# GpSimd instead of SyncE issues the row and result transfers of the experts, with longer rings for rows and weights

## The chip, the cores and the metric

The kernel runs on one core of a Trainium2 chip. The metric is the device time of one execution in microseconds (us). Three runs of the kernel before gave 1716.96 us as the median (1716.13 to 1722.56). The profile is of one more execution, of 1711.19 us, whose traced span is 1709.2 us.

## The reference, cut to what matters

Four layers follow each other on x of shape (4, 512, 128), each adding an attention and a feed-forward part of the normalized x. The last two feed-forward parts are mixtures of experts: a shared expert for all 2048 tokens, and the best 4 of 32 (layer 2) or 2 of 16 (layer 3) routed ones for each token.

```
# layer 2: E = 32 experts of width 96, best 4
act = silu(x @ w_gate[e]) * (x @ w_up[e]);  eo = act @ w_down[e]
routed = sum over the token's 4 experts of combine[t, e] * eo[t, e]
# layer 3: E = 16 experts of width 256, best 2, with biases
h = silu(x @ W1[e] + b1[e]) * (x @ W11[e] + b11[e]);  y += (h @ W2[e] + b2[e]) * gates[t, e]
```

## The kernel before, in words

Each engine has its own program, written out by hand; they meet only through semaphores (`wait_ge`). In layers 2 and 3 all engines walk the same list of steps: `both` counts n, the step of attention, and four quarters i of each; a "slot" below is one such quarter (4n + i). In a slot TensorE makes one 128x512 score tile whose row maximum VectorE takes (L1486), one more whose exponential ScalarE takes (L1927), and part of the product with V. Layer 3's attention starts 64 steps behind that of layer 2. Beside these, `plan` places the expert work in slots, and each engine runs its share of a slot's tasks in the plan's order, so an engine that waits for one task holds up all that stands behind it in its own program.

The expert work goes like this. After routing, GpSimd scatters the normalized tokens by indirect DMA into a DRAM list `xd`, sorted by expert in tiles of 128 rows (L2143; 64 transfers in layer 2, 32 in layer 3). Layer 2 has 96 such tiles, two to an item, layer 3 has 48, one to an item; so each layer has 48 routed items, behind the items of the shared expert. For each routed item:

- "rows": SyncE loads two tiles of `xd` into a buffer of the ring `XG` of 4 pairs (L2377), once the tile that stood there has been transposed (`XTURN`, L2376). The first four pairs are loaded by GpSimd in `first_rows` (L2151), right after the scatter.
- "turned": TensorE transposes the rows (L942), ScalarE copies them out (L1912).
- "hidden": TensorE multiplies with the expert's gate and up weights, which stand in the ring `WR` of 6 items (layer 2) or 5 items (layer 3), numbers held in `ahead` (L371). Then ScalarE and VectorE gate the result (L1906, L1452, L1454).
- "down": TensorE multiplies with the down weights; then SyncE loads the weights of the item `ahead` further on (`item_weights`, L2331; it waits for `DOWN` of this item, reads the expert's number from SBUF, and issues one transfer per tile). ScalarE copies the result to `YOs` (L1918), and SyncE, having waited for that copy (`YO_A`, L2384), writes it to the DRAM list `yd` (L2385).

When all results have landed, GpSimd gathers them back by indirect DMA (L2134) and VectorE adds them to X (L1473).

SyncE's program also holds the loads of the attention: six transfers of `stack` for every four steps (L2260, L2262), and the writes of `split_out` (L2243, L2246), three times a layer for the batches 1 to 3. GpSimd's program also has the scatter, the four operations of `part_of` per batch (L2089 to L2097), and the gathers.

## Time and profile before

| | |
|---|---|
| median of three runs | 1716.96 us (1716.13 to 1722.56) |
| profiled execution | 1711.19 us, span 1709.2 us |
| TensorE matmul busy | 1268.7 us (74%) |
| VectorE busy | 1246.9 us (73%) |
| ScalarE busy | 921.7 us (54%) |
| GpSimd busy | 307.0 us (18%) |

The span falls in stretches with different limits, so the shares over the whole say little about one of them. The routed items of layer 2 run from 918 to about 1090 us, those of layer 3 from 1415 to about 1612 us. SyncE has no busy time in the page; its queue of issued transfers is read from the timeline of engine SP. The chain of work that ended last gives at each step what released it; "DMA RA<-xd" there is a transfer from its issue to its landing.

### The profile page before, as it was taken

The numbers are of one execution on the slowest core, as the hardware profiler recorded it, in microseconds if no ns is written. First come the engines' busy times: TensorE is split into PE (matmuls) and PEld (weight loads), VectorE is DVE, ScalarE is ACT, GpSimd is POOL, SyncE is SP. The second block draws the span as 40 slices with busy tenths as digits, with TensorE's granted clock in tenths as the row PEclk, the third lists the DMA queues.
The fourth block names the chain that finished last, engine by engine and source line by source line (L and its number), as shares of the span: only waits on it lengthen the run. The fifth ranks groups of instructions, "written<-read, shape, count | busy, mean of one in ns | idle before, by whom it ended". The sixth has DMA issues, their size and how long they took to land.

```text
span 1709.2 us, 24192 instructions
## 1 busy us (share of the span) xinstructions
PE 1268.7 (74%) x7198; PEld 678.4 (40%) x7198; DVE 1246.9 (73%) x4139; ACT 921.7 (54%) x2172; POOL 307.0 (18%) x418
## 2 busy tenths in 40 slices
PE   6988979887432334256788999877899879987976
PEld 2444545444211112131145656422565435665522
DVE  5997979988789999868565666667677755544563
ACT  2898988886354444412344556544444445544545
POOL 0111102002000000004654001166110250100051
PEclk6999999899755555556889999988998989998989
DMA  3010101100392000012313666523110234545420
GB/s 114 24 70 6 51 24 32 49 1 1 111 329 81 6 6 11 2 46 86 121 53 100 182 179 180 157 75 64 46 31 27 80 68 140 149 101 159 117 67 23
DMA packets 171850, 135.40 MB, mean 79 GB/s; under 512 B 75218, under 2 KB 149271, under 8 KB 171667
## 3 DMA queue, kind: packets, MB, share of 16 engines
q1 hardware_dynamic: 163561, 119.83, 24.1%
q0 software_dynamic: 6528, 13.64, 2.9%
q8 instruction: 58, 0.95, 0.2%
q14 instruction: 71, 0.58, 0.1%
q10 hardware_dynamic: 1632, 0.39, 0.1%
HBM read 95.96 MB, written 47.27 MB: 84 GB/s over the span
## 4 chain that ended last, share of the span: by engine, by line
PE 41%; DVE 36%; issue 8%; ACT 6%; DMA 4%; SPq 2%; another core or an unknown queue 2%; POOL 1%; DVEq 0%; ACTq 0%
PE PS L575 36%; DVE nmx L1486 6%; DVE RA L1731 6%; DVE RA L1735 4%; PE PS L571 4%; DVE RA L1289 4%; DVE RA L1292 3%; DMA RA<-xd 2%; DMA RA<-wd 1%; DVE RB L1289 1%; ACT RA L1877 1%; PE PS L942 1%; DVE RB L1292 1%; DMA RA<-scr 1%
## 5 line engine op out<-in xcount | busy, mean ns | idle before, releaser
L575 PE MATMUL PS<-RA 125*128 125x512 bf16 (+6 forms) x2368 | 552.2, 347 | 105.2 <-DVE nmx L1486 63.0
L1486 DVE TENSOR_REDUCE nmx<-PS 128x1 f32<-128x512 f32 x512 | 346.4, 684 | 260.7 <-PE PS L575 224.4
L1927 ACT ACTIVATE RA<-PS 128x512 f32<-128x512 f32 x512 | 295.5, 599 | 251.5 <-PE PS L575 200.7
L575 PEld LDWEIGHTS PS<-RA 125*128 125x128 bf16 (+4 forms) x2368 | 230.0, 132 | 372.8 <-DVE nmx L1486 144.3
L575 PE MATMUL PS<-RA,Vs 128*32 128x512 f32 x1240 | 201.6, 646 | 0.7 <-ACT RA L1927 0.7
L2053 ACT ACTIVATE RA<-RA 128x8 f32<-128x8 f32 x511 | 107.5, 210 | 142.5 <-DVE RA L1731 142.3
L571 PE MATMUL PS<-ident,RB 128*128 128x128 f32 (+2 forms) x331 | 61.3, 329 | 157.6 <-DVE RB L1664 141.4
L2134 POOL DMA_INDIRECT RA<-yd,RA x96 | 94.8, 987 | 274.6 <-DMA yd<-RB 217.9
L1289 DVE TENSOR_SCALAR RA<-PS 128x1024 f32<-128x1024 f32 x96 | 116.9, 1218 | 21.9 <-PE PS L575 20.9
L1877 ACT ACTIVATE RA<-RA,nm 128x512 f32<-128x512 f32 x192 | 128.8, 725 | 1.1 <-POOL nm L2208 0.9
L1292 DVE CUSTOM_DVE_ANT_0 RA<-RA,RB 128x512 f32<-128x512 f32 x192 | 125.1, 688 | 3.3
L571 PE MATMUL PS<-ident,RA 128*128 128x128 f32 x768 | 107.8, 285 | 26.3 <-ACT RA L1883 17.5
L571 PEld LDWEIGHTS PS<-ident,RB 128*128 128x128 f32 (+2 forms) x331 | 43.8, 164 | 192.2 <-DVE RB L1664 113.1
L1906 ACT ACTIVATE RA<-PS 128x256 f32<-128x256 f32 (+1 forms) x144 | 55.1, 382 | 112.6 <-PE PS L575 107.0
L2143 POOL DMA_INDIRECT xd<-XN,RA x96 | 93.4, 973 | 123.5 <-DVE sd L1416 52.7
L571 PEld LDWEIGHTS PS<-ident,RA 128*128 128x128 f32 x768 | 89.1, 144 | 61.0 <-ACT RA L1883 28.6
L2089 POOL CAST parts<-QK 128x1024 bf16<-128x1024 f32 x6 | 6.2, 1037 | 549.8 <-DVE ms L1245 549.8
L1731 DVE TENSOR_TENSOR_SCAN RA<-RA 128x16 f32<-128x16 f32 x512 | 95.5, 187 | 7.0 <-ACT RA L2053 1.6
L1735 DVE COPY RA<-RA 128x4 f32<-128x4 f32 x512 | 86.3, 169 | 15.1 <-DVE RA L1731 0.4
L575 PE MATMUL PS<-RB 128*128 128x352 f32 (+2 forms) x88 | 60.2, 842 | 36.7 <-ACT RB L2027 23.3
L575 PE MATMUL PS<-RB,RA 128*96 128x128 f32 (+1 forms) x576 | 83.0, 281 | 2.8 <-DVE RA L1454 2.8
L2208 POOL TENSOR_SCALAR nm<-mx 128x2 f32<-128x2 f32 x128 | 27.3, 214 | 319.7 <-DVE mx L1292 269.7
(308 smaller groups left out, 1923.8 us busy)
## 6 DMA issues: line engine op xcount, KB each, us to landing
RA<-scr SPq DMA_DIRECT2D x288, 96.0 KB
RA<-wd SPq DMA_DIRECT2D x48, 384.0 KB
RA<-wd SPq DMA_DIRECT2D x96, 160.0 KB
xd<-Otok SPq DMA_DIRECT2D x36, 256.0 KB, 3.3
RA<-xd SPq DMA_DIRECT2D x64, 128.0 KB, 3.2
scr<-parts SPq DMA_DIRECT2D x48, 128.0 KB
yd<-RB SPq DMA_DIRECT2D x48, 128.0 KB, 2.7
wd<-in_L_ffn_W SPq DMA_DIRECT2D x2, 2048.0 KB, 14.9
```

The costliest lines, as they stand in the source:

```text
L571: ins = e.transpose(bank[bk][0:s.shape[-1], j * 128:j * 128 + s.shape[0]], s, ident[0:s.shape[0], 0:s.shape[0]])
L575: return e.matmul(o, l, r, start=first, stop=last)
L1289: e.tensor_scalar(Y[n % 4][:, 2 * u:2 * u + 2, :], PS[:, 2 * u:2 * u + 2, :], C0, -C0, ALU.min, ALU.max).then_inc(*CLIP.up("clip", n, u))
L1292: ins = e.tensor_tensor_reduce(out=Y[n % 4][:, qt, :], in0=Y[n % 4][:, qt, :], in1=Dk[:, qt, :], scale=1.0, scalar=NEG, op0=ALU.mult, op1= ...
L1486: e.tensor_reduce(nmx[:, (g + lx) % 3, c:c + 1], bank[(6, 0)[i % 2]], AX.X, ALU.max, negate=True).then_inc(*ROWMAX.up(layer, n, i))
L1731: e.tensor_tensor_scan(sc, RA[:, 16 * t:16 * t + 16], RA[:, 8192 + 16 * t:8192 + 16 * t + 16], 0.0, ALU.mult, ALU.subtract).then_inc(*SCAN ...
L1735: e.tensor_copy(D1[:, t + 1, :, 0], sc.rearrange("p (b e) -> p b e", e=4)[:, :, 2]).then_inc(*CARRY.up(t))
L1877: e.activation(Y[m % 4][:, qt, :], Y[m % 4][:, qt, :], ACT.Exp, bias=nm[:, m % 4, qt:qt + 1]).then_inc(*EXP.up(0, m, qt))
L1927: e.activation(chunk(layer, k, i), bank[(1, 5)[i % 2]], ACT.Exp).then_inc(*EXP.up(layer, k, i))
L2053: e.activation(D1[:, t + 1, :, 1:3], sv[:, :, 3:4].broadcast_to([128, 4, 2]), ACT.Tanh).then_inc(*TANH.up(t + 1))
L2134: e.indirect_dma_start(XG[:, i % 6 // 2, i % 2, :], None, yd[lx], bass.IndirectOffsetOnAxis(ap=IDX[:, n, j:j + 1], axis=0)).then_inc(*GATH ...
L2143: e.indirect_dma_start(xd[lx], bass.IndirectOffsetOnAxis(ap=IDX[:, n, j:j + 1], axis=0), XN[:, n, :], None).then_inc(*SCAT.up(lx, "all"))
```

## The change

GpSimd's `expert_step` takes over the tasks "rows" and the storing half of "down" from SyncE's, with the same waits and the same slots; SyncE keeps the weights. The ring of row pairs grows from 4 to 6 and is filled by six transfers in `first_rows`; the plan asks for rows later in number (the pair 6 ahead of the one freed) in the same slots. The ring of weights grows to 11 items in layer 2 and 9 in layer 3; the added buffers lie in `RB`, and `weights` fills the longer rings at the start of each layer, one task a slot in layer 2 and two in layer 3. The computation is the same.

```diff
-    topk, ntiles, nexps, ffs, groups, ahead = (4, 2), (NT2, NT3), (32, 16), (96, 256), (2, 1), (6, 5)
+    topk, ntiles, nexps, ffs, groups, ahead = (4, 2), (NT2, NT3), (32, 16), (96, 256), (2, 1), (11, 9)
@@ the plan of the expert steps
-            r = G * (i - nsh + 6)
-            fetch = [("rows", r)] if i >= first and end > nsh and r >= 8 and r % 2 == 0 and r < ntiles[lx] else []
+            r = G * (i - nsh) + 12 + 4 * (G - 1)
+            fetch = [("rows", r)] if i >= first and end > nsh and r >= 12 and r % 2 == 0 and r < ntiles[lx] else []
@@ pool_program
         def expert_step(lx, task):
+            if name == "rows":
+                r = task[1]
+                u = r // 2 % 6
+                pool.wait_ge(SCAT, lx, "all")
+                pool.wait_ge(XTURN, lx, nsh + (r - 11) // G)
+                e.dma_start(XG[:, u, :, :], xd[lx][128 * r:128 * r + 256, :].rearrange("(t p) d -> p t d", p=128)).then_inc(*XGIN[u].up(lx, r // 2))
+            elif name == "down" and task[1] >= nsh:
+                i = task[1]
+                r = G * (i - nsh)
+                pool.wait_ge(YO_A, lx, i)
+                e.dma_start(yd[lx][128 * r:128 * r + 128 * G, :].rearrange("(t p) d -> p t d", p=128),
+                            YOs[lx][:, i % 6, :].rearrange("p (t d) -> p t d", d=128)).then_inc(*YOUT[i % 6].up(lx, i))
...
@@ first_rows
-            for u in range(4):
+            for u in range(6):
@@ sp_program
         def expert_step(lx, task):
-            if name == "rows":
...
-            elif name == "down" and task[1] >= nsh:
+            if name == "down" and task[1] >= nsh:
                 i = task[1]
-                r = G * (i - nsh)
                 if i + ahead[lx] < items[lx]:
                     item_weights(lx, i + ahead[lx])
-                sp.wait_ge(YO_A, lx, i)
-                e.dma_start(yd[lx]...
```

## Rows read from the trace of the kernel before

**Rows 1.** Stretches: us, busy PE PEld DVE ACT POOL, clock, DMA share, GB/s

```profile
915.00:1112.00 197.00, 177.37 (x1186) 109.77 (x1186) 118.86 (x282) 111.39 (x265) 16.95 (x17) 0.99 0.60 170
1410.00:1625.00 215.00, 190.64 (x1352) 126.08 (x1351) 115.33 (x267) 106.55 (x272) 9.27 (x8) 0.97 0.48 132
```

**Rows 2.** TensorE's waits, 915 to 1112: waited for, total us, times, longest

```profile
PE PS L942 <- DMA RA<-xd: 7.7, 4, 4.9
```

**Rows 3.** TensorE's waits, 1410 to 1625

```profile
PE PS L575 <- DMA RA<-wd: 7.0, 6, 2.1
PE PS L942 <- DMA RA<-xd: 5.0, 3, 3.9
PE PS L942 <- DVE Otok L1216: 4.3, 4, 1.4
```

**Rows 4.** TensorE's wait for the first rows, 1410 to 1420

```profile
PE PS L942 <- DMA RA<-xd: 0.6, 1, 0.6
```

**Rows 5.** SyncE's queue about 1030: start us, us, line, operation, count

```profile
1025.32 1.19 SPq L2331 DMA_DIRECT2D RA<-wd  x2
1026.57 0.42 SPq L2385 DMA_DIRECT2D yd<-RB  x1
1027.05 0.79 SPq L2260 DMA_DIRECT2D RA<-scr  x1
...
1031.53 0.44 SPq L2377 DMA_DIRECT2D RA<-xd  x1
```

**Rows 6.** The chain that ended last: start us, us, what

```profile
1031.53 7.74 DMA RA<-xd
...
1559.59 8.70 DMA RA<-wd
```

**Rows 7.** TensorE's timeline about 1560, with idle time before and releaser

```profile
1555.06 1.29 PE L575 MATMUL PS<-RA 128*128 128x128 f32 x8 [1.50 <-DMA RA<-wd]
...
1560.71 1.44 PE L575 MATMUL PS<-RA 128*128 128x128 f32 x12
...
1567.51 0.45 PE L942 MATMUL PS<-ident,RA 128*128 128x128 f32 x1 [3.94 <-DMA RA<-xd]
1568.42 2.79 PE L575 MATMUL PS<-RA 128*128 128x128 f32 x12 [0.47 <-DMA RA<-wd]
```

**Rows 8.** Busy time and clock in three stretches of 5 us (columns of rows 1)

```profile
1555.00:1560.00 5.00, 4.94 (x28) 3.18 (x28) 0.94 (x2) 1.77 (x4) 0.00 (x0) 0.66 0.42 137
1565.00:1570.00 5.00, 2.02 (x8) 1.66 (x9) 0.24 (x1) 0.27 (x1) 0.00 (x0) 0.61 0.84 258
1570.00:1575.00 5.00, 5.00 (x28) 3.02 (x28) 1.76 (x4) 2.05 (x5) 0.00 (x0) 0.71 0.30 69
```

**Rows 9.** TensorE's transposes of layer 2's, then layer 3's items: min/median/max ns, first and last

```profile
L942 PE MATMUL PS<-ident,RA x96: 270/273/445, 918.1 to 1087.1; 128*128 128x128 f32 x96
L942 PE MATMUL PS<-ident,RA x48: 272/274/447, 1415.3 to 1610.8; 128*128 128x128 f32 x48
```

**Rows 10.** GpSimd's own transfers, by line: min/median/max ns

```profile
L2151 POOL DMA_DIRECT2D RA<-xd x8: 727/756/807, 915.5 to 1412.9; - x8
...
DMA to landing us min/median/max: 2.5/3.6/6.2
```

**Rows 11.** GpSimd's timeline about 1024: start us, us, operation, idle before

```profile
1024.37 1.03 POOL L2089 CAST parts<-QK 128x1024 bf16<-128x1024 f32 x1 [105.88 <-DVE ms L1245]
...
1028.79 2.13 POOL L2097 TENSOR_TENSOR parts<-QK,parts 128x1024 bf16<-128x1024 f32 x1
```

**Rows 12.** SyncE's queue, at the start of both layers' weights

```profile
833.13 4.89 SPq L2331 DMA_DIRECT2D RA<-wd  x6
844.96 0.76 SPq L2260 DMA_DIRECT2D RA<-scr  x1
...
1356.42 3.78 SPq L2331 DMA_DIRECT2D RA<-wd  x5
```

**Rows 13.** The chain that ended last, between 849 and 860

```profile
849.96 3.35 another core or an unknown queue
854.71 4.33 another core or an unknown queue
```

More of the change, by code:

```diff
@@ L202, in build @@
     SG = RA[:, 8416:8432]
-    XG = RA[:, 8448:9472].rearrange("p (u t k) -> p u t k", u=4, t=2)
-    HB = RA[:, 9728:10240].rearrange("p (u k) -> p u k", u=2)
-    XGTs = (RB[:, 11008:11520].rearrange("p (u k) -> p u k", u=2), RA[:, 9472:9728].rearrange("p (u k) -> p u k", u=2))
-    WR = (RA[:, 18432:22272].rearrange("p (u g k) -> p u g k", u=6, g=2), RA[:, 18432:22272].rearrange("p (u g k) -> p u g k", u=5, g=1))
+    XG = RA[:, 8448:9984].rearrange("p (u t k) -> p u t k", u=6, t=2)
+    HB = RA[:, 10240:10752].rearrange("p (u k) -> p u k", u=2)
+    XGTs = (RB[:, 11008:11520].rearrange("p (u k) -> p u k", u=2), RA[:, 9984:10240].rearrange("p (u k) -> p u k", u=2))
+    WR = ([x[:, i:i + 640].rearrange("p (g k) -> p g k", g=2) for x, a, n in ((RA, 18432, 6), (RB, 6944, 5)) for i in range(a, a + 640 * n, 640)],
+          [x[:, i:i + 768].rearrange("p (g k) -> p g k", g=1) for x, a, n in ((RA, 18432, 5), (RB, 9216, 4)) for i in range(a, a + 768 * n, 768)])
     YOs = (RB[:, 0:1536].rearrange("p (u k) -> p u k", u=6), RB[:, 5504:6272].rearrange("p (u k) -> p u k", u=6))
@@ L246, in build @@
     W2S, W3S, TABLE = loads("w2s"), loads("w3s"), loads("table")
-    WIN = [loads(f"win{i}") for i in range(6)]
+    WIN = [loads(f"win{i}") for i in range(11)]
     B3, SEL, B2IN, B2UP, B2DN, B3UP, B3DN = (loads(n) for n in ("b3", "sel", "b2in", "b2up", "b2dn", "b3up", "b3dn"))
@@ L252, in build @@
     SCAT = loads("scatter")
-    XGIN = [loads(f"xg{i}") for i in range(4)]
-    XGFIRST = [loads(f"xgfirst{i}") for i in range(4)]
+    XGIN = [loads(f"xg{i}") for i in range(6)]
+    XGFIRST = [loads(f"xgfirst{i}") for i in range(6)]
     YOUT = [loads(f"yout{i}") for i in range(6)]
@@ L911, in expert_step @@
                 else:
-                    w = WR[lx][:, (i - nsh) % ahead[lx], :, :]
+                    w = WR[lx][(i - nsh) % ahead[lx]]
                     pe.wait_ge(WIN[(i - nsh) % ahead[lx]], lx, i)
@@ L937, in expert_step @@
                     r = G * (i - nsh) + g
-                    if r < 8:
+                    if r < 12:
                         pe.wait_ge(XGFIRST[r // 2], lx)
                     else:
-                        pe.wait_ge(XGIN[r // 2 % 4], lx, r // 2)
-                    ins = e.transpose(bank[2][:, 128 * g:128 * g + 128], XG[:, r // 2 % 4, r % 2, :], ident[:, :])
+                        pe.wait_ge(XGIN[r // 2 % 6], lx, r // 2)
+                    ins = e.transpose(bank[2][:, 128 * g:128 * g + 128], XG[:, r // 2 % 6, r % 2, :], ident[:, :])
                 ins.then_inc(*XTURN.up(lx, i))
@@ L961, in expert_step @@
                         lhs = HB[0:m, i % 2, 128 * (nc_ * g + c):128 * (nc_ * g + c) + 128]
-                        w = shared[lx][i][3][c] if i < nsh else WR[lx][0:m, (i - nsh) % ahead[lx], g, 2 * f + 128 * c:2 * f + 128 * c + 128]
+                        w = shared[lx][i][3][c] if i < nsh else WR[lx][(i - nsh) % ahead[lx]][0:m, g, 2 * f + 128 * c:2 * f + 128 * c + 128]
                         ins = mm(o, lhs, w, c == 0 and lx == 0, c == nc_ - 1)
@@ L2121, in expert_step @@
             name, k = task[0], topk[lx]
-            if name == "gather":
+            nsh, G = len(shared[lx]), groups[lx]
+            if name == "rows":
[4 more added lines that the diff above has]
+                e.dma_start(XG[:, u, :, :], xd[lx][128 * r:128 * r + 256, :].rearrange("(t p) d -> p t d", p=128)).then_inc(*XGIN[u].up(lx, r // 2))
+                XGIN[u].mark(lx, "all")
+            elif name == "down" and task[1] >= nsh:
[4 more added lines that the diff above has]
+                            YOs[lx][:, i % 6, :].rearrange("p (t d) -> p t d", d=128)).then_inc(*YOUT[i % 6].up(lx, i))
+                YOUT[i % 6].mark(lx, "all")
+            elif name == "gather":
                 i = task[1]
@@ L2149, in first_rows @@
                 pool.wait_ge(XW, "routed", 0, 16 * topk[0] - 1)
-            for u in range(4):
+            for u in range(6):
                 e.dma_start(XG[:, u, :, :], xd[lx][256 * u:256 * u + 256, :].rearrange("(t p) d -> p t d", p=128)).then_inc(*XGFIRST[u].up(lx))
@@ L2370, in expert_step @@
             name = task[0]
[L2371 to L2379 removed]
+            nsh = len(shared[lx])
+            if name == "down" and task[1] >= nsh:
                 i = task[1]
[L2381 removed]
                 if i + ahead[lx] < items[lx]:
                     item_weights(lx, i + ahead[lx])
[L2384 to L2387 removed]
         xin = T["L0_attn_x"].rearrange("b s d -> (b s) d").rearrange("(n p) d -> p n d", p=128)
```

12 lines of the change are left out of this document (1 added, 11 removed).

## The prediction

> **What bounds the kernel now.** I read first the busy time by stretch [rows 1]. The two stretches in which the routed items run, 915 to 1112 and 1410 to 1625 us, have TensorE busy 177.4 of 197 and 190.6 of 215 us, at a granted clock of 0.99 and 0.97, while VectorE and ScalarE are busy 50 to 60% of either and GpSimd 17 and 9 us in all. So TensorE sets the pace there, and what can be won without less matmul work is its idle time: 19.6 and 24.4 us. These stretches hold all that the change moves, apart from the first loads.
>
> Next I read what TensorE waited for in them [rows 2, 3]. The reader is to see two kinds of rows. Waits for a transfer: 7.7 us for rows (RA<-xd) in layer 2; 7.0 us for weights (RA<-wd) and 5.0 us for rows in layer 3. And waits for other engines, such as 4.3 us for Otok in layer 3 which the change doesn't touch. Not all row waits are SyncE's: the longest of layer 2, 4.9 us, is the one for the first rows (GpSimd's first row load starts at 915.5, the first transpose at 918.1) [rows 2, 9, 10], and 0.6 us in layer 3 is the same [rows 4]. Both come out of the scatter and `first_rows`, which are GpSimd's already.
>
> Why are SyncE's transfers late? Its queue about 1030 us shows it [rows 5]. One item costs it 0.44 us for rows, 1.19 us for two weight transfers and 0.42 us for the result, and then the six loads of `stack` follow in its program, from 1027.05 to 1031.53, 4.48 us in which nothing of the experts is issued. The row load at 1031.53 stands right behind. The chain of work has this very transfer on it for 7.74 us, and one of weights in layer 3 for 8.70 us [rows 6]: it lands slowly since stack loads of the same queue are ahead of it, and SyncE comes back to the items late. The ring of 4 pairs and the ring of 5 weights are too short for such a delay and landing together.
>
> **The change part by part.**
>
> 1. Row loads leave SyncE's queue and are asked for 6 pairs ahead. An item of layer 2 takes (1087.1 - 918.1)/47 = 3.60 us, one of layer 3 (1610.8 - 1415.3)/47 = 4.16 us [rows 9]. Six pairs are about 21 us of lead in layer 2, where one pair is one item; in layer 3, where a pair serves two items, the load is asked for ten items before its use, about 41 us. The longest landing of GpSimd's own eight row loads is 6.2 us [rows 10]. That covers it several times. Gone: in layer 2, 7.7 - 4.9 = 2.8 us; in layer 3, 5.0 - 0.6 = 4.4 us.
>
> 2. Weights stay with SyncE, 11 and 9 items ahead, which is 39 and 37 us of lead against a burst of about 4.5 us plus a landing of 8.7 [rows 5, 6]. The writes of `split_out` hold SyncE too, in groups of at most six transfers, which would have to take 20 us each time to use up that lead. Gone: 7.0 us in layer 3 [rows 3]; in layer 2 no weight wait stands among TensorE's waits.
>
> 3. The clock. Within 1553 to 1568 us TensorE waited for a weight and for a row, and right behind it the granted clock is 0.66, 0.61 and 0.71, a mixture of the full 2.4 GHz and of 1.2 GHz [rows 8]. Twelve matmuls that take 1.44 us before the stall take 2.79 us behind it [rows 7]. The work that a full clock would have saved is busy time by what is missing: 4.94 x 0.34 + 2.02 x 0.39 + 5.00 x 0.29 = 1.7 + 0.8 + 1.5 = 3.9 us. The fall followed these waits, so it goes with them.
>
> 4. GpSimd's new work: 60 row loads, 96 results and 4 more first rows, 160 instructions at 0.756 us [rows 10] and a gap of about 0.3, some 170 us, in stretches where it is busy 17 and 9 us [rows 1]. In layer 2 one item costs it 2 x 1.06 = 2.1 of 3.60 us. Cover holds unless an issue takes more than 1.5 us. The page of rows has no case above 0.807 us for this kind.
>
> 5. The waits that GpSimd now has. `XTURN` and `YO_A` tie it to the slots; behind them stand its own next tasks: `part_of` for batch 3. Before, these four ran in one go as soon as VectorE's maximum was there, from 1024.37 to 1030.9 [rows 11]; now they stand in four slots four apart, 12 slots, some 27 us, from first to last. The write that needs them comes three slots behind the last, and behind a stack burst of 4.5 us. I cost this at nothing; if the cover fails, it is one SyncE wait of about 3 us that no weight with 39 us of lead feels. Who waits for GpSimd's results is ScalarE's copy six items later (21 us) and the first gather. Cost 0, from 0 to 3 us.
>
> 6. The longer first fill: five more items in layer 2 and four in layer 3. At 4.89/3 = 1.63 us an item SyncE is busy until 833.13 + 8 x 1.63 = 846.2 where its next stack load stood at 844.96; in layer 3, 9 x 3.78/5 = 6.8 us from 1356.42, so until 1363.2 [rows 12]. The load delayed by 1.2 us is wanted some 16 slots later. But two pauses of 3.35 and 4.33 us stand on the chain there with an unknown releaser [rows 13]; the first comes right behind the burst of six stack loads that begins at 844.96. 1.6 MB more about 840 us might bring one more or lengthen one, or shift them off. Bounds -4 to +8 us, value taken 0, since the second comes with no burst right before it.
>
> The sum: 2.8 + 4.4 + 7.0 + 3.9 = 18.1 us off. Since TensorE is the bound before and behind each stall, I let nothing be taken back by the next wait; that is the optimistic end, and half is the other (9 us). The profiled execution would go from 1711.19 to 1693.1 us (span 1709.2 to 1691.1). It lies 5.8 us below the median of the three runs, so on the median: 1716.96 - 18.1 = 1698.9, rounded to 1699.
>
> A page speaks against the change. GpSimd's row loads were issued in 0.727 to 0.807 us each while VectorE ran its reductions from PSUM [rows 10]. The Trainium skill, page "SBUF — State Buffer", section "SBUF: two separate sides", says that a transfer issued by GpSimd has its descriptors written by GpSimd's cores, which are shut out while VectorE runs an SBUF-to-SBUF operation in its fast mode on two ports; its advice is to issue from SyncE or ScalarE. By that rule alone the change would be a loss. The operations that VectorE runs in these stretches read PSUM or are tiny, and the trace's eight loads and their spread of 80 ns show nothing of such a lock.
>
> **The rivals.**
>
> A. Others take back the stall (chance 0.20). While TensorE waited for a row, Otok and the gates were finishing too; 4.3 us of Otok waits remain in layer 3 [rows 3], and they may grow when TensorE arrives earlier. For it: each slot has a round trip to VectorE. Against it: VectorE is idle for 40% of both stretches. Half the gain stays: 1717 - 9 = 1708, just at the edge of what counts as no change.
>
> B. The first fill brings pauses (0.13). Two more pauses of the kind in rows 13 cost 2 x 4.3 = 8.6 us, four cost 17 (one for each burst of the two fills, and one behind each): 1708 to 1716.
>
> C. GpSimd becomes the bound (0.07), the slower side. Place: the 48 items of layer 2. Price: if one issue costs as much as GpSimd's longest operation in the row, 2.13 us [rows 11], with the gap 2.43, an item costs it 4.86 against 3.60 us: 48 x 1.26 = 60 us, less the 21.6 us that six buffers absorb, 38 us. Layer 3 has one and a half issues an item, 3.65 below 4.16, and keeps its gain of 15. Time: 1716.96 + 38 - 15 = 1740. It decides from 1.5 us an issue. The lock of the page above would act here. Against it: rows 10.
>
> D. The change doesn't do what it says would need that the waits come from full transfer engines and not from the queue; the DMA share is 0.60 and 0.48 [rows 1], so over some 37 us of lead it can't last. I put it into A.
>
> **How the numbers follow.** Forecast (0.60): all four terms, 1699, its own range 1694 to 1706. A 0.20 at 1708, B 0.13 at 1708 to 1716, C 0.07 at 1740. The range takes A and B whole and a few us of spread of the median (its three runs span 6.4 us), and leaves out C: 1690 to 1718. A measurement of this kernel can tell about 0.5%, 8.6 us. Faster by more: the forecast and part of A and B, 0.66. Within: the rest of A and B, 0.25. Slower: C and a rest, 0.09.
>
> **What would show it.** In the profile after: TensorE's waits for RA<-wd gone in the second stretch, those for RA<-xd left with the first rows alone (about 5 and 0.6 us); no clock below 0.9 about 1550 to 1575; GpSimd busy 50 to 70 us more in each of the two stretches, with row loads of 0.75 us; SyncE waiting for DOWN in front of most weights. The stretch of layer 2 shorter by 3 us, that of layer 3 by 15. The prediction is wrong if issues take over 1.5 us, if Otok waits grow by the same sum, or if the stretch from 820 to 870 us gets longer.

## The result, and the profile after

The changed kernel takes 1698.28 us as the median of six runs (1695.56 to 1703.93); six runs of the kernel before, taken beside them and before them, have 1716.55 us (1711.11 to 1722.56). The ratio is estimated from all these runs at 0.9889, with an interval of 0.9868 to 0.9911 (the quotient of the two medians alone is 0.9894): faster by 18.3 us. The forecast was 1699 us. One run of the kernel before, in the third series below, took 2111.86 us in a slow state, and the ratios leave it out.

| | before | after |
|---|---|---|
| median of six runs | 1716.55 us | 1698.28 us |
| profiled execution, its span | 1711.19, 1709.2 us | 1701.65, 1699.9 us |
| TensorE matmul busy | 1268.7 us | 1257.0 us |
| VectorE, ScalarE busy | 1246.9, 921.7 us | 1249.4, 921.7 us |
| GpSimd busy | 307.0 us | 413.1 us |
| layer 2's items, first to last transpose | 169.0 us | 169.9 us |
| layer 3's items, first to last transpose | 195.5 us | 179.0 us |

The two profiled executions differ by 9.5 us only, half of what the medians do: that of before lay 5.4 us below its median, that of after 3.4 us above. So the sum of the prediction must be read against the stretches, not against the two spans. Lines of the kernel after stand one or 16 lower than before: L942 is now L943, SyncE's weight loads L2347, GpSimd's row loads L2129 and results L2135, and the first rows L2167.

TensorE's waits of the kernel after, in the same two windows as [rows 2, 3], 915 to 1112 and 1410 to 1625 us (waited for, total us, times, longest):

```profile
PE PS L943 <- DMA RA<-xd: 5.2, 1, 5.2
PE PS L943 <- DVE Otok L1217: 4.3, 3, 2.2
...
PE PS L943 <- DVE Otok L1217: 4.8, 4, 1.4
PE PS L576 <- DVE nmx L1487: 4.2, 2, 3.9
...
PE PS L576 <- DMA RA<-mT: 0.4, 1, 0.4
```

In layer 2 one wait for rows is left, the one for the first rows. In layer 3 no wait for rows or weights stands in the answer; the only transfer waited for is one of mT, 0.4 us. The wait of 3.9 us for nmx (a row maximum) isn't at the items: it ends at 1413.5, ahead of the first transpose of layer 3. The transposes themselves (duration ns min/median/max, first and last start), to be laid beside [rows 9]:

```profile
L943 PE MATMUL PS<-ident,RA x96: 270/273/449, 921.4 to 1091.3; 128*128 128x128 f32 x96
...
L943 PE MATMUL PS<-ident,RA x48: 272/274/477, 1423.4 to 1602.4; 128*128 128x128 f32 x48
```

An item of layer 3 takes 179.0/47 = 3.81 us where it took 4.16; one of layer 2 takes 169.9/47 = 3.61, as before. Busy time and clock of the kernel after in the stretches of [rows 1] and in four of 5 us (columns: PE, PEld, DVE, ACT, POOL busy, clock, DMA share, GB/s):

```profile
915.00:1112.00 197.00, 177.94 (x1157) 111.06 (x1175) 116.06 (x274) 108.71 (x259) 84.69 (x109) 0.97 0.51 154
1410.00:1625.00 215.00, 195.61 (x1382) 127.66 (x1409) 124.43 (x289) 113.89 (x287) 58.69 (x86) 0.98 0.46 131
...
1555.00:1560.00 5.00, 4.95 (x38) 3.21 (x38) 3.87 (x8) 3.23 (x9) 1.80 (x3) 1.00 0.58 119
...
1565.00:1570.00 5.00, 5.00 (x41) 3.56 (x42) 3.19 (x7) 3.04 (x9) 1.08 (x2) 1.00 0.80 223
1570.00:1575.00 5.00, 4.30 (x38) 3.49 (x41) 2.88 (x10) 2.29 (x9) 0.54 (x1) 1.00 1.02 299
```

TensorE stays at the full 2.4 GHz where the kernel before had 0.66, 0.61 and 0.71 [rows 8]. GpSimd's busy time in the two stretches went from 17 and 9 us to 85 and 59. Its transfers, of the kernel after (duration of one on GpSimd's queue, ns min/median/max, then the landings of the rows and of the results):

```profile
L2129 POOL DMA_DIRECT2D RA<-xd x60: 712/720/750, 922.9 to 1562.8; - x60
...
DMA to landing us min/median/max: 2.5/3.6/6.5
...
L2135 POOL DMA_DIRECT2D yd<-RB x96: 538/650/731, 934.4 to 1611.9; - x96
...
DMA to landing us min/median/max: 1.8/3.4/6.6
```

A row load takes 0.720 us of GpSimd where the prediction, from eight of them, took 0.756, and the spread over 60 is 38 ns. The Trainium skill, page "DMA: Bandwidth & Descriptors", section "Anatomy of one DMA — SWDGE (gpsimd) path", gives a fit for a transfer issued by GpSimd of 2.0 us and the bytes at 436 GB/s; 128 KB would be 2.3 us by it, an estimate. The trace has 2.5 us for the fastest of these 60, 3.6 in the median and 6.5 for the slowest: here the fit lies just under the fastest, and a lead has to be sized by the slowest.

### The profile page after: what moved, and what is told of

It reads as the page before. It is cut to its first block, busy times and chain, and to the rows that moved or that the text cites. A ratio compares the mean times of both kernels' runs of the same rounds, so it can differ in the third digit from the quotient of the medians.

```text
span 1699.9 us, 24108 instructions
## 1 busy us (share of the span) xinstructions
PE 1257.0 (74%) x7112; PEld 673.3 (40%) x7198; DVE 1249.4 (74%) x4139; ACT 921.7 (54%) x2172; POOL 413.1 (24%) x578
## 4 chain that ended last, share of the span: by engine, by line
PE 43%; DVE 37%; issue 7%; ACT 6%; another core or an unknown queue 3%; DMA 2%; POOL 1%; SPq 1%; ACTq 0%; DVEq 0%
PE PS L576 38%; DVE nmx L1487 6%; DVE RA L1732 6%; DVE RA L1736 4%; PE PS L572 4%; DVE RA L1290 4%; DVE RA L1293 3%; DVE RB L1290 1%; PE PS L943 1%; DVE RB L1293 1%; ACT RA L1878 1%; DVE Otok L1217 1%; ACT RA L1928 1%; DVE RA L1455 1%
## 5 line engine op out<-in xcount | busy, mean ns | idle before, releaser
L576 PE MATMUL PS<-RA 128*128 128x512 bf16 (+6 forms) x1963 | 505.7, 354 | 104.6 <-DVE nmx L1487 69.1
L576 PEld LDWEIGHTS PS<-RA 128*128 128x128 bf16 (+4 forms) x2048 | 193.9, 122 | 367.2 <-DVE nmx L1487 148.5
L576 PE MATMUL PS<-RA,Vs 128*32 128x512 f32 x1240 | 205.2, 657 | 3.5 <-ACT RA L1928 1.0
L572 PE MATMUL PS<-ident,RA 128*128 128x128 f32 x768 | 107.1, 284 | 26.5 <-ACT RA L1884 17.7
L2135 POOL DMA_DIRECT2D yd<-RB x96 | 61.1, 637 | 202.3 <-ACT RB L1919 199.1
L576 PE MATMUL PS<-RB 128*96 128x128 f32 (+3 forms) x248 | 83.1, 484 | 34.5 <-ACT RB L2028 21.1
```

Of the source, the lines that this page charges most:

```text
L572: ins = e.transpose(bank[bk][0:s.shape[-1], j * 128:j * 128 + s.shape[0]], s, ident[0:s.shape[0], 0:s.shape[0]])
L576: return e.matmul(o, l, r, start=first, stop=last)
```

## The experiments

The question that the result leaves is which half of the change does it. Theory 1 (that of the prediction): a transfer comes late because it stands in SyncE's queue behind others, and what removes the wait is lead, so the rings decide and the issuer matters little. Theory 2: the issuer decides, since GpSimd has a queue with nothing else in it. The kernels ran in three series. The kernel before had medians of 1670.72 us in the first (26 runs), 1718.99 in the second (20) and 1670.01 in the third (11), so only ratios within a series are compared; what differs between the series is told at the end. As above, a ratio is an estimate from all runs of both kernels, and need not be the quotient of the two medians.

| kernel | issuer of rows, results | rings: pairs, weights, results | us | ratio, interval |
|---|---|---|---|---|
| series 1: after_again | GpSimd | 6, 11/9, 6 | 1651.61 | 0.9890 (0.9862 to 0.9919) |
| rings_alone | SyncE | 6, 11/9, 6 | 1658.73 | 0.9920 (0.9891 to 0.9948) |
| issuer_alone | GpSimd | 4, 6/5, 6 | 1664.67 | 0.9963 (0.9940 to 0.9987) |
| weights_ring_alone | SyncE | 4, 11/9, 6 | 1666.71 | 0.9988 (0.9962 to 1.0015) |
| series 2: before_again | SyncE | 4, 6/5, 6 | 1716.54 | 0.9992 (0.9973 to 1.0011) |
| rings_results | SyncE | 6, 11/9, 6/10 | 1692.01 | 0.9849 (0.9822 to 0.9876) |
| later_rows | GpSimd | 6, 11/9, 6 | 1706.15 | 0.9927 (0.9901 to 0.9953) |
| filler3 | GpSimd, with more work | 6, 11/9, 6 | 1735.36 | 1.0087 (1.0056 to 1.0118) |
| series 3: after_third | GpSimd | 6, 11/9, 6 | 1650.19 | 0.9897 (0.9873 to 0.9920) |
| rings_results_again | SyncE | 6, 11/9, 6/10 | 1647.17 | 0.9875 (0.9841 to 0.9909) |
| gpsimd_results_ring | GpSimd | 6, 11/9, 6/10 | 1652.21 | 0.9905 (0.9884 to 0.9927) |
| gpsimd_results_only | SyncE rows, GpSimd results | 6, 11/9, 6 | 1650.10 | 0.9878 (0.9850 to 0.9906) |

What these kernels spend where, from the first and last starts of three lines in each profile. The first column of times is from VectorE's first row maximum of layer 2's attention to the first transpose of layer 2's rows; then layer 2's items, first to last transpose; then the stretch between, from there to the first transpose of layer 3's rows; then layer 3's items; last, from the last transpose of layer 3 to the end of the span:

```
                       to layer 2's items   items 2   between   items 3   behind
before                       161.9           169.0     328.2     195.5     98.4
after                        167.7           169.9     332.1     179.0     97.5
after_again                  147.7           170.1     309.4     180.4     86.6
rings_alone                  146.8           172.8     307.5     187.1     87.8
issuer_alone                 146.9           170.6     302.9     193.9     87.4
weights_ring_alone           145.8           171.3     311.4     193.5     86.0
before_again                 161.1           172.5     325.0     196.9     99.4
rings_results                160.6           170.1     325.5     179.2     98.8
later_rows                   169.2           169.0     334.4     181.8     96.7
filler3                      165.2           195.7     343.1     178.5     96.0
after_third                  146.5           170.1     304.6     179.7     87.4
rings_results_again          148.7           170.3     301.1     180.1     87.3
gpsimd_results_ring          148.8           170.5     308.0     180.0     87.5
gpsimd_results_only          147.0           169.9     311.7     179.9     88.0
```

### after_again: the change once more, beside its halves

No edit: the kernel after.

> The changed kernel once more, for a second profile. Its first profile is only 9.3 us shorter than that of the kernel before, the medians differ by 18.3 us. In it the items of layer 3 gave 16.5 us, but the stretch from the first score tile of layer 2 to its first routed transpose took 167.7 instead of 161.9 us, and the items of layer 2 took 169.9 instead of 169.0 us. Theory 1 (the loss in the first stretch is the price of the longer first fill of weights): 166 to 169 us again, with pauses of an unknown releaser of together about 15 us between 820 and 870. Theory 2 (such pauses fall differently in every execution, and the profiles were a long and a short one): the stretch lies anywhere from 160 to 168 us. The ratio to the kernel before is 0.989 in both.

Measured 1651.61 us, 0.9890: the ratio is that of the first measurement, though all kernels are some 46 us shorter here. The stretch to layer 2's items took 147.7 us, which neither theory had: there are no pauses in this profile, as the last section tells. The items of layer 3 take 180.4 us. This is the yardstick of the series.

### rings_alone: the longer rings, SyncE still issues everything

```diff
 pool_program, expert_step
-            if name == "rows":
...
 sp_program, expert_step
+            if name == "rows":
+                sp.wait_ge(XTURN, lx, nsh + (r - 11) // G)
+                e.dma_start(XG[:, u, :, :], xd[lx]...
+            elif name == "down" and task[1] >= nsh:
+                sp.wait_ge(YO_A, lx, i)
+                e.dma_start(yd[lx]...
```

> The longer rings (6 pairs, 11 and 9 weights) with SyncE as the issuer of rows and results, as before. Theory 1 (the stall is SyncE's burst plus a slow landing against too little lead; lead cures it by itself): TensorE's waits for weights 0 and for rows only the first ones (about 5 us and 0.6 us), items of layer 3 in 179 to 182 us, ratio 0.989 to 0.991. Theory 2 (what matters is that SyncE's queue is too full, so that it falls behind for good): row waits of over 2 us stay in layer 2, layer 3's items above 186 us, ratio 0.994 or more.

Measured 1658.73 us, 0.9920: most of the gain, but the items of layer 3 take 187.1 us and not 180.4. Theory 1 is right about the waits for rows and weights and wrong about the items, for which theory 2 has the right number (above 186 us) and not the reason. TensorE's waits in layer 3, 1372 to 1570 us, have no wait for weights, and for rows only the first; a new one stands beside it. The rows below are, in turn, TensorE's waits, ScalarE's wait about 1525 to 1550, two copies of ScalarE, two stores of SyncE, and TensorE's timeline behind:

```profile
PE PS L943 <- DMA RA<-xd: 4.1, 1, 4.1
PE PS L576 <- ACT RB L1919: 4.1, 1, 4.1
...
ACT RB L1919 <- DMA yd<-RB: 6.4, 2, 5.7
...
1513.35 0.27 ACT L1919 COPY RB<-PS 128x128 f32<-128x128 f32 x1 [0.17 <-PE PS L576]
...
1539.38 0.27 ACT L1919 COPY RB<-PS 128x128 f32<-128x128 f32 x1 [5.74 <-DMA yd<-RB]
...
1517.82 3.19 SPq L2248 DMA_DIRECT2D scr<-parts  x2
...
1532.16 0.41 SPq L2387 DMA_DIRECT2D yd<-RB  x1
...
1539.70 2.82 PE L576 MATMUL PS<-RA 128*128 128x128 f32 x12 [4.08 <-ACT RB L1919]
```

The copy at 1513.35 is the 31st of layer 3, and the store at 1532.16 is the 31st of SyncE: a result was finished at 1513.62 and stood for 18.5 us before SyncE came to it, behind the writes of `split_out`, the six stack loads and the tasks that these had put off. The 37th copy needs that place, since the ring has 6. It comes at 1539.38, 7.2 us behind the issue. So a third ring became the shortest. The twelve matmuls behind this wait take 2.82 us, as in the stall of the kernel before [rows 7].

Layer 2's items take 2.7 us more here than in after_again, with the same waits of TensorE but for the first rows (4.9 and 5.3 us). There the granted clock differs: what it lacks costs 7.6 us here and 4.5 in after_again, by the working of "3, the clock" below.

### issuer_alone: GpSimd issues, the rings as before

```diff
-    ... groups, ahead = ..., (2, 1), (11, 9)
+    ... groups, ahead = ..., (2, 1), (6, 5)
-            for u in range(6):
+            for u in range(4):
 (and % 4 for % 6 where the pairs are counted)
```

> GpSimd issues rows and results, the rings stay 4 pairs, 6 and 5 items. Theory 1 (lead): the waits for rows go, since the load is no longer behind the stack burst and lands in at most 6.2 us against 14 us of lead; the waits for weights in layer 3 stay in part, 2 to 5 us of 7.0, since SyncE's bursts still stand before them; items of layer 3 in 183 to 189 us, ratio 0.992 to 0.995. Theory 2 (the queue): both kinds of waits go, 179 to 182 us, ratio 0.989.

Measured 1664.67 us, 0.9963. TensorE's waits in layer 3, 1372 to 1570 us, and the longest of them:

```profile
PE PS L576 <- DMA RA<-wd: 8.0, 4, 5.6
PE PS L943 <- DMA RA<-xd: 4.4, 1, 4.4
...
1530.08 2.79 PE L576 MATMUL PS<-RA 128*128 128x128 f32 x12 [5.61 <-DMA RA<-wd]
```

With rows and results gone from its queue SyncE is still late with the weights: 8.0 us of waits against 7.0 before [rows 3]. All row waits but the first are gone. A shorter queue alone doesn't do what lead does. Theory 1 had the kinds of waits right and was too hopeful in all its numbers (2 to 5 us of weight waits, 183 to 189 us of items, 0.992 to 0.995, where 8.0, 193.9 and 0.9963 were measured).

### weights_ring_alone: only the ring of weights is longer

```diff
 against the kernel before:
-    ... groups, ahead = ..., (2, 1), (6, 5)
+    ... groups, ahead = ..., (2, 1), (11, 9)
```

> Only the rings of weights are longer (11 and 9 items); 4 pairs of rows, SyncE issues all. Theory 1 (lead): waits for weights 0, waits for rows stay at 2.8 us in layer 2 and 4.4 us in layer 3 beside the first ones; items of layer 3 in 186 to 190 us, ratio 0.993 to 0.996. Theory 2 (the rows were late because of the weights' own waits in the queue): row waits go as well, ratio 0.989 to 0.991.

Measured 1666.71 us, 0.9988: no gain that can be told. The same view, same window:

```profile
PE PS L943 <- DMA RA<-xd: 17.7, 5, 6.7
```

The waits for weights are gone, and the waits for rows behind the first have grown from 4.4 us (5.0 less 0.6, [rows 3, 4]) to 11.0 (17.7 less the 6.7 of the first rows). Weights and rows together were 7.0 + 4.4 = 11.4 us in the kernel before, so nearly nothing is gone. The delay in SyncE's queue is one; whichever ring is the shortest shows it. That is a new wait in the place of the one removed, and neither theory had it (theory 1: 4.4 us of row waits, 186 to 190 us of items, 0.993 to 0.996, where 193.5 us and 0.9988 were measured). It is why half a change was worth next to nothing: GpSimd as issuer alone is worth 0.4%, the weights' ring alone 0.1%, both rings alone 0.8%, everything 1.1%. The ring of pairs alone wasn't run. Nor was the plan alone: in layer 3 the kernel before asks for a row load four items before its use (`G * (i - nsh + 6)`), where the changed one asks ten before, and its four pairs were free two items earlier than it asked. So some 8 us of the new lead of the rows there could have been had without a longer ring; what they are worth isn't known.

### before_again: the kernel before, profiled in the second series

No edit. It gives series 2 a profile of the kernel before.

> The kernel before once more, for a profile from the same chip as its variants. Theory 1 (the pauses of unknown releaser belong to the chip and not to the change): they are there or missing in this profile as in the others of its chip, and the stretches outside the routed items agree with the changed kernel's within 2 us each; the items of layer 3 take 193 to 197 us with 10 to 14 us of waits for transfers besides the first rows. Theory 2 (the change's longer first fill or GpSimd's transfers cause or lengthen them): the stretch up to layer 2's first transpose is 3 us or more shorter here than in the changed kernel. Ratio 1.000.

Measured 1716.54 us, 0.9992. Its items take 172.5 us in layer 2, where the first profile of the same kernel has 169.0. So the same kernel differs by 3.5 us in this stretch from one execution to the next, more than the 2.8 us that step 1 forecast for it. Layer 3's 196.9 us are within theory 1's 193 to 197, and the stretch to layer 2's items, 161.1 us, is within a microsecond of the first profile of this kernel. It is 6.6 us shorter than in the kernel after, and that is the sign of theory 2. rings_results below, with the long fill and 160.6 us, clears the fill of it; the rest of the question is for the last section.

### rings_results: SyncE issues everything, and the ring of results is longer too

```diff
 against rings_alone:
-    YOs = (..., RB[:, 5504:6272].rearrange("p (u k) -> p u k", u=6))
+    YOs = (..., RB[:, 5504:6784].rearrange("p (u k) -> p u k", u=10))
+    yring = (6, 10)
-                if i - nsh >= 6:
-                    act.wait_ge(YOUT[i % 6], lx, i - 6)
+                k = yring[lx]
+                if i - nsh >= k:
+                    act.wait_ge(YOUT[i % k], lx, i - k)
```

> SyncE issues everything, as before, with the longer rings of rows and weights, and layer 3's ring of results is lengthened from 6 to 10 as well. In the profile of the long rings without it, the one wait left was ScalarE's for a result's landing (5.7 us, passed on to TensorE as 4.1 us). Theory 1 (each stall is the shortest lead among the three rings, whoever issues): that wait goes, layer 3's items take 179 to 183 us instead of 187, ratio 0.988 to 0.991, so that GpSimd as the issuer is not needed. Theory 2 (GpSimd as the issuer has a worth of its own): another wait takes its place, 185 to 188 us, ratio 0.991 to 0.994.

Measured 1692.01 us, 0.9849. Its layer 3 items take 179.2 us, as in the kernel after, with GpSimd doing nothing for them. The rows are TensorE's wait for transfers in layer 2 (916.5 to 1090 us) and the first two rows of its waits about layer 3's items (1400 to 1590 us). The 5.0 us of "issue" lie ahead of the first transpose, which starts at 1412.1; among the items one transfer is still waited for, a weight, for 0.2 us:

```profile
PE PS L944 <- DMA RA<-xd: 5.0, 1, 5.0
...
PE PS L577 <- issue: 5.0, 2, 4.3
PE PS L944 <- DVE Otok L1218: 3.4, 3, 1.4
```

The comparison with before_again is the cleanest of all, since both are of one series and their other stretches agree within 1.1 us: items of layer 2 shorter by 2.4 us, of layer 3 by 17.7, the spans by 21.1 (1711.2 to 1690.1). Theory 1 stands: once all three rings have lead, the issuer isn't needed. The ratio is better than its range (0.988 to 0.991).

### later_rows: the change, with the first rows wanted three slots later

```diff
+            if not lx and i == nsh - 2:
+                steps += [[] for _ in range(4)]
-    last = spread(2, expert_steps(0, 0), 68, 1.15)
+    last = spread(2, expert_steps(0, 0), 68, 1.2)
-    last = spread(3, expert_steps(1, 1), READY3[3] + 71 - 4 * LEAD, 1.05)
+    last = spread(3, expert_steps(1, 1), READY3[3] + 74 - 4 * LEAD, 1.05)
```

> The changed kernel with the first routed transposes three slots later in both layers (four empty steps and a rate of 1.2 instead of 1.15 in layer 2, a start of 74 instead of 71 in layer 3), because the first rows are what is left of TensorE's waits for transfers: 5.3 and 6.2 us. Theory 1 (TensorE has attention work to do in those three slots): both waits fall under 1.5 us, ratio 0.982 to 0.986 to the kernel before, that is 5 to 10 us better than the change. Theory 2 (the slots behind are as full and only the wait moves): the waits are gone but the stretches give it back, ratio 0.988 to 0.990.

This goes for the 5.2 us that are left. Measured 1706.15 us, 0.9927: no gain beside the change, if anything a loss, and outside the ranges of both theories. In layer 2, 920 to 1095 us, TensorE waited

```profile
PE PS L578 <- DVE RA L1457: 5.3, 12, 0.5
...
PE PS L945 <- DMA RA<-xd: 3.2, 1, 3.2
```

so the first-row wait fell by 2.0 us only, and the waits for the gates (L1457, L1455 of the kernel after, 1.7 us there in its items) grew by 3.6, since the items are packed closer. In layer 3 the kernels after and later_rows have no first-row wait at all in these profiles, so there the idea had nothing to gain; the items of later_rows took 181.8 us against 179.0. Moving the start gave nothing.

### filler3: the change, with more work on GpSimd in layer 2

```diff
                 r = G * (i - nsh)
+                if lx == 0:
+                    for _ in range(3):
+                        pool.wait_last(BIAS_P)
+                        e.memset(RB[:, 3840:4864], 0.0).then_inc(*BIAS_P.up())
                 pool.wait_ge(YO_A, lx, i)
```

It only adds work: three fills of an unused 128x1024 piece for each of layer 2's 48 items.

> The changed kernel with three memsets of 128x1024 (about 1 us each) on GpSimd ahead of each result of layer 2. GpSimd's work for an item rises from about 2.0 to about 5.1 us, against 3.62 us that TensorE takes. Theory 1 (rival C of the prediction: it becomes the bound once an item costs it more than TensorE, less what the rings absorb): 48 x 1.5 = 72 us less about 21 us, layer 2's items in 215 to 240 us instead of 170, ratio to the kernel before 1.01 to 1.04. Theory 2 (GpSimd's pace matters less, since rows are asked for ahead): under 190 us, ratio below 1.003.

Measured 1735.36 us, 1.0087. The fills, then GpSimd's timeline, busy time over 170 us, and TensorE's and ScalarE's waits in layer 2:

```profile
L2137 POOL MEMSET RB<- x144: 952/952/985, 935.4 to 1145.2; 128x1024 f32 x144
...
1004.97 0.73 POOL L2139 DMA_DIRECT2D yd<-RB  x1
1005.70 0.72 POOL L2129 DMA_DIRECT2D RA<-xd  x1
1006.42 2.99 POOL L2137 MEMSET RB<- 128x1024 f32 x3
1009.36 0.73 POOL L2139 DMA_DIRECT2D yd<-RB  x1
...
940.00:1110.00 170.00, 141.47 (x913) 91.92 (x928) 93.98 (x212) 87.43 (x211) 164.68 (x191) 0.95 0.50 149
...
PE PS L943 <- DMA RA<-xd: 18.4, 9, 5.4
...
ACT RB L1919 <- DMA yd<-RB: 19.1, 9, 4.5
```

GpSimd is busy 164.7 of 170 us and needs 1009.36 - 1004.97 = 4.39 us an item, more than the 3.60 us of TensorE: it is the bound. The items of layer 2 take 195.7 us, 25.8 more than after, and from their last transpose to VectorE's first addition of a gathered result it is 32.9 us and not 24.7, 8.2 more, 34 us in all. The expectation of theory 1 had 215 to 240 us for the items, theory 2 below 190; it came out between, as did the ratio (1.01 to 1.04, and below 1.003). The fills made an item cost 4.39 us and not the 5.1 that theory 1 had. By its own working 48 x (4.39 - 3.60) = 38 us are lost, less about 21 us that the rings absorb, 17 us; 34 were measured, so the rings absorbed some 4 us only. One of them, the results' ring of 6, makes ScalarE wait for 19.1 us here. So rival C is a real mechanism here, and the change is away from it: in the kernel after, GpSimd is busy 67.2 of the 160 us from 930 to 1090, that is 1.5 us for each item of 3.6. It would take 2.1 us more an item, or 1.05 us more on each of the two issues.

### Series 3: after_third, rings_results_again, gpsimd_results_ring, gpsimd_results_only

These four ask whether SyncE with three long rings really beats GpSimd, and if so, which of GpSimd's two tasks costs it.

```diff
 after_third: no edit. rings_results_again: as rings_results.
 gpsimd_results_ring: the kernel after, with yring = (6, 10) as in rings_results
 gpsimd_results_only: the kernel after, with only the task "rows" back in sp_program
```

> The changed kernel again, beside the kernel with the longer ring of results that SyncE serves, in one series. Theory 1 (both have no wait for transfers left but the first rows, and what differs between single profiles outside the routed items is pauses of unknown releaser): ratio 0.987 to 0.991, layer 3's items 178 to 181 us, and the difference to the other kernel is within 0.3%. Theory 2 (GpSimd as the issuer costs something outside the items): 0.4% or more behind the other kernel again, with the stretch from the first score tile to layer 2's first transpose 4 us or more longer than the other's.

> SyncE issues everything, rings of 6 pairs, 11 and 9 weights and 10 results in layer 3, again. Its first ratio was 0.9849 (0.9822 to 0.9876), that of the change 0.9889. Theory 1: 0.986 to 0.989, within 0.3% of the changed kernel. Theory 2: 0.983 to 0.986, 0.4% or more better than the changed kernel.

> The changed kernel with the longer ring of results in layer 3 too (10 instead of 6). No wait for a result's landing was seen in the changed kernel, so by theory 1 (the shortest lead decides, and none is short here any more) nothing changes: within 0.2% of the changed kernel. Theory 2 (the ring of results has a worth of its own, whoever issues, and is what made the other kernel better): 0.3% or more better than the changed kernel.

> The long rings of rows and weights, SyncE issues rows and weights, GpSimd the results alone, with their ring of 6. Theory 1 (with the long rings the only lead too short at SyncE is that of the results): ScalarE's wait for a result's landing is gone, layer 3's items take 179 to 182 us as in the changed kernel, ratio 0.985 to 0.990. Theory 2 (SyncE with rows is still too full): waits for rows or weights of over 2 us, items above 184 us, ratio 0.991 or more.

Measured 0.9897, 0.9875, 0.9905 and 0.9878. The items take 169.9 to 170.5 us in layer 2 and 179.7 to 180.1 in layer 3 in all four: they are the same kernel there. The intervals overlap. The longer ring of results gives GpSimd nothing (0.9897 and 0.9905), as it should where no store is late. SyncE for all is ahead of the change by 0.4% in series 2 (against the ratio of the first measurement) and by 0.2% in series 3, and both are within what such a measurement can tell. The two profiles of series 3 differ by 4.6 us (1646.5 and 1641.9), none of it in the items; 3.5 us are in the stretch between. But that stretch has anything from 301.1 to 311.7 us in the eight profiles of series 1 and 3, with either issuer, so it tells nothing for or against GpSimd. It is left open. What is shown is that, with three long rings, GpSimd as issuer gains nothing that can be told over SyncE, and that rings_results is at least as good as the kernel after, with the lowest ratio in both series.

## Why the prediction was right

The forecast of 1699 us was 0.7 us off the median of 1698.28. For the profiled execution it had a span of 1691.1 us, and that was 1699.9: as the execution of before was 5.4 us below its median and that of after 3.4 above, the single spans hide half of the gain, and only the stretches and the later series show which steps held. That four terms came out at 18.1 us beside 18.3 measured is in part luck: the interval of the ratio alone is 7 us wide, and between two profiles of one kernel layer 2's items differ by up to 3.5 us.

**1, the row waits.** Layer 2: from 7.7 to 5.2 us, 2.5 gone where 2.8 were forecast, and what is left is the first wait, as said. Layer 3: from 5.0 to none. Its 0.6 us of first rows [rows 4] went too, but pauses of 5.5 and 4.6 us right before it had put everything off.

**2, the weights.** 7.0 us to none, as forecast. SyncE now waits for `DOWN`, 64.0 us in layer 2 and 67.9 in layer 3, as the last part of the prediction wanted. As a sign this is weaker than it looks: in layer 3 SyncE waited 67.9 us for `DOWN` before the change too, and in layer 2 7.2 us. So its queue in layer 3 isn't full, it is held up now and then. weights_ring_alone shows that this term and the row waits need each other: with the weights' ring alone the 7.0 us came back as row waits. The prediction treated the terms as a sum; the runs show a pair. The sum was right because both parts were there.

**3, the clock.** In layer 3 it held. In windows of 5 us through the items, busy time times what the clock lacks is about 5.2 us before and 1.1 after (these sums move by up to 0.8 us with where the windows are laid): some 4 us, where 3.9 were forecast. In layer 2 the prediction had looked for no such loss, and it is what ate the gain of step 1: by the same working about 1.5 us before, 4.3 us after, of which 2.7 stand behind the wait for the first rows and 1.6 behind one for Otok. The rows are the windows with the largest losses of the kernel after, and the answering ones of the kernel before, with the wait ahead of each second one:

```profile
918.00:923.00 5.00, 4.88 (x27) 3.56 (x28) 0.55 (x2) 1.35 (x3) 0.49 (x1) 0.70 0.37 114
988.00:993.00 5.00, 4.97 (x37) 3.03 (x36) 2.72 (x9) 3.07 (x8) 0.00 (x0) 1.00 0.46 126
...
986.81 0.44 PE L942 MATMUL PS<-ident,RA 128*128 128x128 f32 x2 [2.23 <-DVE Otok L1216]
```

```profile
921.00:926.00 5.00, 4.57 (x23) 3.19 (x23) 0.35 (x1) 1.35 (x3) 2.65 (x4) 0.50 0.91 286
991.00:996.00 5.00, 4.67 (x24) 2.86 (x25) 0.88 (x4) 1.72 (x4) 1.45 (x2) 0.66 0.18 44
...
991.33 0.44 PE L943 MATMUL PS<-ident,RA 128*128 128x128 f32 x2 [2.23 <-DVE Otok L1217]
```

The same wait of 2.23 us for Otok stands in both kernels. In one the clock falls to 0.66 behind it, in the other it stays at 1.00. It isn't the change: before_again has 4.1 us of such losses in layer 2 and rings_results 4.6, and between these two the items got shorter by 2.4 us. Less these losses the items take 167.5 and 168.4 us in the two profiles of the kernel before, 165.6 after and 165.5 in rings_results: 1.9 to 2.9 us less. So the term of 2.8 us for layer 2 was about right in size and can't be seen in one pair of profiles, since the clock alone scatters by 2.6 us between two profiles of the same kernel. The step's layer 2 half is the one that the first pair of profiles contradicts (169.0 to 169.9 us) and the second bears out.

**4, GpSimd's new work.** Hidden, as forecast. 160 new issues: 60 x 0.720 + 96 x 0.637 + 4 x 0.75 = 107 us, and its busy time rose by 106.1. The prediction's 170 us had a gap of 0.3 us behind each issue, which needn't be there: in filler3's timeline the next issue starts at 1004.97 + 0.73 = 1005.70. Per stretch 67.7 and 49.4 us more, where 50 to 70 were forecast. The rule of the Trainium skill, page "SBUF — State Buffer", section "SBUF: two separate sides", by which the change would be a loss, would show here as issues that take far longer than the others. The largest of the 156 is 0.750 us, with VectorE busy for 116.06 of 197 and 124.43 of 215 us: nothing here looks like the lock. The prediction's own evidence was thinner than it says: VectorE stood idle for the 6.10 us before 921.27, in which the four row loads of layer 2 were issued, and only the four of layer 3 had its reductions beside them. Whether VectorE ran in the mode that the rule names isn't in the trace, so the rule itself isn't tested.

**5, the new waits of GpSimd.** The cost was nothing, as said. The rows of the kernel after are, in turn, the first and last operation of `part_of` for batch 3, SyncE's only wait for such an operation in the window 915 to 1112, and its first writes of batch 3:

```profile
1034.67 1.05 POOL L2090 CAST parts<-QK 128x1024 bf16<-128x1024 f32 x1
...
1056.06 2.15 POOL L2098 TENSOR_TENSOR parts<-QK,parts 128x1024 bf16<-128x1024 f32 x1
...
SPq L2259 <- POOL parts L2098: 10.3, 1, 10.3
...
1065.13 1.23 SPq L2259 DMA_DIRECT2D scr<-parts  x2
```

The four spread over 23.5 us (27 were forecast). The wait of 10.3 us isn't for them: it ends at 918.58, and is for batch 2, whose last operation GpSimd had at 916.43, behind the scatter and ahead of the first rows, as before the change. For batch 3 SyncE came to the write only at 1065.13, behind its stack loads, 6.9 us after the parts were done, and no wait for them stands in 925 to 1112. The prediction allowed for one of 3 us.

**6, the longer first fill.** SyncE's queue of the kernel after, beside [rows 12]:

```profile
833.28 6.20 SPq L2347 DMA_DIRECT2D RA<-wd  x6
840.91 8.79 SPq L2347 DMA_DIRECT2D RB<-wd  x10
849.72 0.73 SPq L2276 DMA_DIRECT2D RA<-scr  x1
```

The next stack load comes at 849.7 where 846.2 was forecast: the first six loads took 6.20 us and not 4.89, the ten into `RB` 0.88 us each and not 0.82, and 1.4 us lie between. In the first profile the stretch to layer 2's items is 5.8 us longer, which looked like rival B: the longest pieces without a releaser on the chain ahead of them sum to 11.9 us before (827.70, 849.96 and 854.71) and 17.2 us after, which are

```profile
827.89 2.76 another core or an unknown queue
839.14 3.27 another core or an unknown queue
851.47 5.85 another core or an unknown queue
864.65 2.96 another core or an unknown queue
907.78 2.31 another core or an unknown queue
```

Without pauses the fill costs nothing. In series 1, kernels with the long fill (after_again, rings_alone, weights_ring_alone) need 147.7, 146.8 and 145.8 us to layer 2's items, and the one with the short fill (issuer_alone) 146.9. In series 2, with pauses, rings_results with the long fill needs 160.6, before_again 161.1. The value 0 was right, and the fill isn't what makes or lengthens the pauses.

**The rivals.** A (others take back the stall): Otok went from 4.3 to 4.8 us in layer 3, and stayed at 4.3 in layer 2; next to nothing. What took back 2.8 us in one profile was the clock in layer 2, which A doesn't name. B: the long fill brings no pause in series 1 and no longer ones in rings_results; why the disturbed profiles with GpSimd as issuer are the longest ones is open, as the last section tells. C: not reached, shown by filler3 to be real. Its price of 38 us for 4.86 us an item was too low: its working took off 21.6 us for the buffers, and filler3's 34 us for 4.39 us an item leave some 4 us for them. By that the price would be about 56 us, an estimate. D: its premise is partly true in the moment, since from 1559.6 to 1568.3 us, while the weights of [rows 6] took 8.70 us to land, the DMA share was 0.92. But rings_results removes, with the same transfers, all waits for rows and weights but the first rows' and one of 0.2 us, so lead covers that too.

**Where the explanation was incomplete.** "Both rings are too short for delay and landing together" was the right cause, but the prediction counted two rings, and there were three. The results' ring of 6 was never named as a risk while SyncE issues them. In the change it was GpSimd that protected it: 187.1 us of layer 3 items against 180.4, 6.7 us, and gpsimd_results_only (179.9 us) shows that giving it the results alone is enough. Nothing else that the new issuer does shows in the runs. Four more places in the ring do the same.

## What to carry to other kernels

A queue that is held up now and then delays everything behind it by the same time, so each ring fed or emptied by it needs lead for the longest delay and a landing; lengthening one moves the wait to the shortest of the others, and the whole gain comes only when the last is long enough. Before a queue is split between two engines, count its rings: here buffers alone did the work of the second issuer. A term of a few us in one stretch should be looked for in two profiles of each kernel, since the clock behind an unchanged wait falls in one and not in the other.

## What the runs showed of the hardware

The granted clock isn't fixed by the wait in front of it: 2.23 us for Otok are followed by 0.66 in one execution and by 1.00 in another.

VectorE stands still for 2 to 6 us at places where the chain names no releaser, and TensorE and ScalarE finish what they have and stop too (1119.19 to 1124.90 of the kernel before: TensorE busy for 0.58 us, VectorE 0.01, ScalarE 0.37). The pieces of about 2 us and more sum to 29 us in the first profile of the kernel before and 46 us in that of after; in the eight profiles of series 1 and 3 no such piece on the chain is longer than 0.79 us. In all six profiles that have them, each such piece of 2 us or more lies where GpSimd issues its indirect transfers, the scatter or the gathers (0.95 us each; in the kernel before 804.7 to 912.4, 1100.1 to 1205.8, 1347.4 to 1407.3 and 1625.3 to 1672.7 us), and none among the routed items. The eight quiet profiles, those of series 1 and 3, have the same indirect transfers without pauses, so these alone don't make them. With pauses the stretch to layer 2's items is 160.6 to 169.2 us in all six profiles of the first measurement and series 2, and 145.8 to 148.8 in all eight others, whatever the kernel. That may be what sets the medians of 1719 and 1670 us apart, but no run tells what makes these pauses, nor why the kernels with GpSimd as issuer have 165 to 169 us there in the disturbed profiles while the others have 160.6 to 161.9 (in filler3 the chain lists none of its pauses there). Without pauses this difference isn't there (146.5 to 148.8 against 145.8 to 148.7), and the change's ratio is 0.9889 with pauses and 0.9890 and 0.9897 without, so it is nothing that the change costs by itself; more was not tried.
